# A depthwise-and-FFT block on one core: the rounding of x and layer 1's additions moved from engines into DMAs

## What is computed

```python
def layer0(x):
    xh = conv1x1(gn(x), w_in, b_in)                  # 128 -> 256 channels
    hcx = relu(mean(xh, points) @ kg_w1.T + kg_b1)   # per image
    k = (hcx @ kg_w2.T + kg_b2)                      # per image: a 3x3 kernel for each of 256 channels
    y = mish(depthwise3x3(xh, k))
    return conv1x1(y, w_out, b_out)                  # 256 -> 128
def layer1(x):                                       # fft over channels, mask, two 128x128 maps, ifft, relu
    return relu(real(ifft(complex(amp_map(fft(x) * mask), phase_map(...)))))
x = x + layer0(x)
x = x + layer1(gn(x))
```

## Time and profile before

| | |
|---|---|
| median of the runs | 3897.72 us |
| profiled execution | 3897.35 us, its span 3895.3 us |
| TensorE busy | 3759.3 us, 97% |
| VectorE busy | 3525.0 us, 90% |
| ScalarE busy | 3448.4 us, 89% |
| GpSimd busy | 2632.5 us, 68% |
| DMA engines busy | 29.5% for the one queue that SyncE issues to |

### The profile page before, as it was taken

One profiled execution on the slowest core, in us unless ns is written; L12 is line 12 of the kernel. 1 busy time (PEld: TensorE's weight loads), 2 busy tenths in 40 slices (PEclk: granted clock), 3 DMA queues, 4 the chain that ended last, 5 costly groups with the idle time before them and its releaser, 6 DMA issues.

```text
span 3895.3 us, 65845 instructions
## 1 busy us (share of the span) xinstructions
PE 3759.3 (97%) x22348; PEld 2259.9 (58%) x22348; DVE 3525.0 (90%) x4778; ACT 3448.4 (89%) x5604; POOL 2632.5 (68%) x2132
## 2 busy tenths in 40 slices
PE   4899999999999999999999999999999999999998
PEld 2555655656555555555556555565655556556554
DVE  5899989899998989989899898998989899899996
ACT  4988999898998989989899998999989999898875
POOL 3456676776767767677777767767677776777763
PEclk8999999999999999999999999999999999999999
DMA  3112333333233333333333332333333233231223
GB/s 139 64 46 85 109 108 110 103 109 114 98 114 103 109 109 105 113 104 109 103 112 111 104 110 102 112 111 103 109 104 113 105 109 111 103 113 71 74 73 124
DMA packets 111292, 401.86 MB, mean 103 GB/s; under 512 B 13232, under 2 KB 14320, under 8 KB 110704
## 3 DMA queue, kind: packets, MB, share of 16 engines
q1 hardware_dynamic: 110960, 397.66, 29.5%
HBM read 263.39 MB, written 134.22 MB: 102 GB/s over the span
## 4 chain that ended last, share of the span: by engine, by line
PE 77%; ACT 7%; POOL 4%; issue 3%; DVE 2%; ACTq 0%; POOLq 0%
PE psA L657 35%; PE psBO L703 19%; PE psL L712 9%; PE psBO L681 2%; PE psBO L683 2%; PE psBO L682 2%; ACT tprod L413 2%; POOL tsum L1110 2%; PE psBO L692 1%; ACT XS L454 1%; PE psBO L694 1%; PE psBO L693 1%; ACT xh L386 1%; PE psA L666 1%; DVE accS L924 1%
## 5 line engine op out<-in xcount | busy, mean ns | idle before, releaser
L657 PE MATMUL psA<-hi,wa 128*128 128x288 f16 (+4 forms) x9792 | 1938.6, 280 | 0.8 <-DVE wtmp L881 0.8
L912 DVE SCALAR_TENSOR_TENSOR accB<-xh,vectors,accB 128x1024 f32<-128x1024 f32 x1280 | 1640.1, 1281 | 0.0
L1110 POOL TENSOR_TENSOR tsum<-tsum,tprod 128x1024 f32<-128x1024 f32 x512 | 1210.6, 2364 | 315.9 <-ACT tprod L413 315.9
L924 DVE SCALAR_TENSOR_TENSOR accS<-side,vectors,accS 128x448 f32<-128x448 f32 x2048 | 1398.6, 683 | 24.1 <-ACT accS L422 14.9
L657 PE MATMUL psA<-lo,wa 128*128 128x288 f16 (+5 forms) x4896 | 1322.0, 280 | 0.0
L657 PEld LDWEIGHTS psA<-hi,wa 128*128 128x128 f16 x9792 | 926.8, 98 | 328.7 <-issue 63.0
L703 PE MATMUL psBO<-wm,woutt 128*128 128x512 f32 x2048 | 963.2, 593 | 3.6 <-DVE X L934 2.1
L1114 POOL TENSOR_TENSOR X<-X,zt 128x512 f32<-128x512 f32 x480 | 612.4, 1276 | 464.3 <-DVE accB L912 394.7
L1102 POOL TENSOR_TENSOR lo<-X,hi 128x1024 f16<-128x1024 f32 x256 | 547.6, 2139 | 359.2 <-ACT hi L371 356.9
L703 PEld LDWEIGHTS psBO<-wm,woutt 128*128 128x128 f32 x2048 | 386.5, 190 | 482.4 <-issue 481.0
L413 ACT ACTIVATE tprod<-xh,vectors 128x1024 f32<-128x1024 f32 x512 | 583.6, 1140 | 31.4 <-POOL tsum L1110 29.4
(11 more groups left out here) (166 smaller groups left out, 3434.6 us busy)
## 6 DMA issues: line engine op xcount, KB each, us to landing
X<-in_x_dram SPq DMA_DIRECT2D x256, 512.0 KB, 3.3
out_dram<-X SPq DMA_DIRECT2D x256, 512.0 KB, 2.6
XS<-in_x_dram SPq DMA_DIRECT2D x240, 512.0 KB, 3.3
X<-in_w_t_dram SPq DMA_DIRECT2D x2, 1152.0 KB, 17.6
w1t<-in_w_t_dram SPq DMA_DIRECT2D x1, 256.0 KB, 2.8
wint<-in_w_in_t_dram SPq DMA_DIRECT2D x1, 128.0 KB, 2.3
woutt<-in_w_out_t_dram SPq DMA_DIRECT2D x1, 128.0 KB, 2.8
wm<-in_cos_m_dram SPq DMA_DIRECT2D x1, 64.0 KB, 4.1
```

The lines of the kernel that those rows point to most:

```text
L657: last = mm(o[:, r:r + q, 0:cols], w, src[:, at:at + q, SIDE + dx - 1:SIDE + dx - 1 + cols], start=(tap == ORDER[0] and w is wh and src is ...
L912: V.scalar_tensor_tensor(out=rows_of(accB[:]), in0=xh[:, 8 * j + dy:8 * j + dy + 8, dx:dx + W], scalar=kk[i % 2][:, TAPS + k:TAPS + k + 1] ...
L924: V.scalar_tensor_tensor(out=side_out(), in0=side[:, 8 * j + dy:8 * j + dy + 8, dx:dx + SIDE], scalar=kk[i % 2][:, k:k + 1], in1=side_out( ...
L1110: P.tensor_tensor(tsum[:], tsum[:], tprod[:], ALU.add).then_inc(s_ta, 1)
```

## The change

Four things are changed.

1. `hi` is no longer made by ScalarE. GpSimd issues a DMA (`high`) that reads the strip from memory once more and rounds it to float16 on the way into `hi`. ScalarE's `cast` is gone.
2. GpSimd's `cast`, which makes `lo`, is done for strip n+3 in place of n+2, and stands behind the second `tap_add` of the slot in place of behind the first `add`. Three strips are done ahead of the loop.
3. GpSimd's `add` becomes a DMA that adds `zt` to the stored strip in memory. SyncE's `store` therefore comes three slots after the strip, as soon as the residual is done; `load_x` waits for the store and for layer 1's matmul. `relu` waits for the landing of the accumulation of the strip before.
4. The building of the next image's weights is set one strip earlier up to the kernels, and its matmuls change banks: group means at strip 9, root at 10, pooled products and hidden layer at 11, kernels at 12 (in `small_1`), bias rows at 14 (in `small_0`), one spread in each of 13, 14 and 15 (in `small_1`). `pool_bias` stands behind `tap_add` and `high`. Seven slots in place of six carry two statistics strips.

```diff
 def stat_strips(n):
-    if n < 6:
+    if n < 7:
         return (2 * n, 2 * n + 1)
-    return (n + 6,) if n + 6 < STATS else ()
+    return (n + 7,) if n + 7 < STATS else ()
...
 def load_x(n):
     ...
         eng.wait_ge(s_out[m % 4], 16 * (m // 4 + 1))
+        eng.wait_ge(s_lm, 2 * m + 2)
...
 def store(m):
-    eng.wait_ge(s_add, 2 * m + 2)
+    eng.wait_ge(s_x1, 2 * m + 2)
...
-                if n >= LAG1 + 1:
-                    store(n - LAG1 - 1)
+                if 3 <= n < N - STRIPS + 3:
+                    store(n - 3)
...
 def relu(m, t):
     ...
     if m >= 1:
-        eng.wait_ge(s_add, 2 * m + t - 1)
+        eng.wait_ge(s_acc[t], 16 * m)
...
+def high(n):
+    b, s, j = n // STRIPS, n % STRIPS, n % 4
+    if n >= 3:
+        eng.wait_ge(s_cv, 2 * (n - 3) + 1)
+    if n >= 4:
+        eng.wait_ge(s_xm, 3 * (n - 4) + 3)
+        eng.wait_ge(s_lo, n - 3)
+    eng.dma_start(hi[:, 8 * j:8 * j + 8, :].rearrange("p r c -> p (r c)"),
+                  x[b, :, s * SP:(s + 1) * SP]).then_inc(s_hi[j], 16)
...
 def add(m, t):
+    b, at = m // STRIPS, m % STRIPS * SP + t * TP
     eng.wait_ge(s_re, 2 * m + t + 1)
-    P.tensor_tensor(half(m, t), half(m, t), zt[:, t, :], ALU.add).then_inc(s_add, 1)
+    eng.wait_ge(s_out[m % 4], 16 * (m // 4 + 1))
+    eng.dma_start(out[b, :, at:at + TP], zt[:, t, :], accum_op=ALU.add).then_inc(s_acc[t], 16)
...
 # GpSimd's slot(n)
     if m >= 1:
         add(m - 1, 1)
-    if n + 2 < N:
-        cast(n + 2)
     ...
     if n + 1 < N:
         tap_add(n + 1, 1)
+    if n + 3 < N:
+        high(n + 3)
+    if s == 11 and build:
+        pool_bias(b + 1)
     if m >= 0:
         add(m, 0)
     if n + 1 < N:
         for k in range(2, EXTRA + 1):
             tap_add(n + 1, k)
+    if n + 3 < N:
+        cast(n + 3)
+    if s == 9 and build:
+        variance("x", b + 1, s_px)
     if s == 10 and build:
-        variance("x", b + 1, s_px)
-    if s == 11 and build:
         rstd("x", b + 1, s_px)
         fold(b + 1)
     ...
     if s == 2 and b >= 1:
         rstd("1", b - 1, s_p1)
         fold_1(b - 1)
```

## The result

| | before | after |
|---|---|---|
| median of the runs | 3897.97 us | 3945.65 us |
| profiled execution's span | 3895.3 us | 3945.0 us |
| VectorE, ScalarE, GpSimd busy | 90%, 89%, 68% | 93%, 82%, 67% |
| DMA engines busy, bytes moved | 0.29, 102 GB/s | 0.64, 151 GB/s |

The changed kernel is slower: the ratio is 1.0125, with an interval of 1.0107 to 1.0142. That is +48 us where +30 was forecast, and inside the range.

The account below looks back on a forecast made before the run. TensorE was taken to bound the ordinary slot at 14.15 us. Per-batch terms +28, the loop +3, additions +2 and first image −3 made +30 on 3897.35, so 3927 us; range for 8 in 10 runs 3885 to 4085.

Parts of the forecast that it names:

- What bounds the kernel: Ordinary slots: TensorE is busy for all 14.15 us, so taking work from ScalarE or GpSimd can't shorten them.
- GpSimd's order: `cast` ahead of the inverse root makes it 2.13 us later; TensorE waits: strip 3 +1.05, strip 11 +1.37.
- the wait for `pool_bias`: Before the hidden-layer matmul: `pool_bias` behind `tap_add` and a DMA issue costs +0.6 us, or nothing for d of 0.4 or less.
- The size of the waits: Strips 3, 12, 13, mostly before the side product: 4.0 us per batch, 59 us or 1.5% at most to gain.
- The small products: Moving the kernel matmuls to strip 12 saves strip 13's 1.85 us; bias rows at strip 14 add 0.7 us.
- The issue price d: GpSimd's time to issue one DMA, three per slot: taken as 1.0 us, within 0.33 to 2.13.
- the loop: From VectorE's first tap through GpSimd's sums, two issues and `cast` back: 12.17 + 2d, passing 14.15 at d = 0.99; +3 us.
- The first rival: The loop binds ordinary slots, with issue at 1.3 us or landing at 4.9: 4040 us, chance 0.27.
- The lock between VectorE and GpSimd: VectorE's first tap and GpSimd's `cast` do not run side by side: the whole 2.13 us charged, possibly only 1.4.
- Additions as DMAs: 480 GpSimd additions of 1.27 us become DMAs: DMA engines 0.64 busy, room enough; +2 us behind the loop.
- Start and first image: Startup roundings cost 0, up to +4 us; first image −3, five slots 0.94 shorter and a seventh statistics slot +1.9.
- The rival of the relief: ScalarE's relief decides if GpSimd reaches the root no later than now: waits go, −48 us, 3850 us; chance 0.10.

Follow-up runs that it names:

- e4: The kernel before with only the rounding DMA for the upper half of x in place of ScalarE's rounding; 3855.11 us, ratio 0.9885.
- the lengthened kernel: The changed kernel with five tiny GpSimd operations between the rounding and first accumulation issues in strips 4 to 8; 4025.23 us, ratio 1.0340.
- e7: e2 with five tiny GpSimd operations added between the same two issues in strips 4 to 8; 3858.62 us, ratio 0.9904.
- e2: The changed kernel with GpSimd's lower-half pass back behind the slot's first accumulation, for strip n+2; 3863.32 us, ratio 0.9907.
- e1: The changed kernel with the inverse root and fold put ahead of GpSimd's lower-half pass at strips 2 and 10; 3866.43 us, ratio 0.9915.

## Why the prediction was right, and where it was off

The forecast's way and most of its terms held; the result lies 18.7 us above it because one term was missing, and one of the agreements is luck in part.

- **What bounds the kernel**: held. Ordinary slots stayed at 14.15 us in every kernel whose loop was not lengthened, whatever ScalarE, VectorE, GpSimd and the DMA engines had to do.
- **GpSimd's order**: held. The root was forecast 2.13 us later with TensorE standing for it in both places; TensorE stood 2.08 and 2.07 us. Strip 3 was to be +1.05 and was +1.0 where the clock held. Strip 11 was to be 1.37 + 0.6 above the strip 12 of before (1.97) and was 18.03 - 16.11 = 1.92. That agreement is luck in part: the relief taken off, 0.76, was 0.46 by e4, and the wait for `pool_bias` before the hidden layer's matmul, put at 0.6, was 0.15 us of idle at most in these 14 images; the two errors nearly cancel.
- **The term that was missing** is the clock behind the stall: 19.9 us at strip 3 and 2.9 at strip 11. I priced an idle TensorE at the idle time and no more. In the trace of before no such stall stood in an ordinary image, so no row showed it. These 22.8 us are more than the whole difference between forecast and result (18.7); without them the span would have grown by 26.9, against +30. That the time still lies inside the range is owed to the range's width.
- **The size of the waits**: read from slot lengths they came to 4.0 us per batch, 59 us in all. The rounding DMA alone took away 0.95 + 0.46 + 1.48 = 2.9 us and left no idle above 0.15 us in those strips, so some 43 us was the most, and the other quarter was no wait.
- **The small products**: strip 13's wait went; by e4 it was 1.48 and not 1.85. The 0.7 us for the bias rows at strip 14 did not come: strip 14 took 15.29 with no idle listed, 0.2 less than before, with one spread less in it. The wait is there without ScalarE's relief, at 1.0 rather than the 1.6 that I had (1.08 + 0.55), and the 0.94 covers it. Strips 9 to 15 together were to be +0.8 per image and were +0.5 without the clock (9.9 - 2.9 = 7.0, over 14).
- **The issue price d**: taken as 1.0 with bounds of 0.33 and 2.13. The line views of the changed kernel, rounding and accumulation (ns min/median/max):

```profile
L1084 POOL DMA_DIRECT2D hi<-in_x_dram x256: 577/612/749, 12.3 to 3838.0; - x128
...
DMA to landing us min/median/max: 3.5/4.1/12.1
```

```profile
L1109 POOL DMA_DIRECT2D out_dram<-zt x480: 853/895/960, 362.7 to 3900.4; - x160
...
DMA to landing us min/median/max: 3.8/4.9/8.0
```

  Two issues are 1.5 us, not 2.0, so the loop is 13.7 by my terms (13.5 by the lengthened kernel) and the 3 us for it fell away. The landing of 4.1 us leaves 9.85 + 4.1 = 13.95, just inside the slot. The first rival was closer than its time suggests: 0.65 us more in the loop and it binds. The Trainium skill, "DMA: Bandwidth & Descriptors", section "Latency and other measured facts", gives about 1 us to first byte for GpSimd's path. No view here shows a first byte; for the price of an issue on the engine the measured 0.61 and 0.90 decide.
- **The lock between VectorE and GpSimd**: charged in full, and the tap does wait for nearly all of the pass (in the lengthened loop it ends 1.10 us past the pass's end, and takes 1.28 alone). The Trainium skill, "SBUF — State Buffer", section "SBUF: two separate sides", says that a VectorE operation with two SBUF inputs, such as the tap, and a GpSimd operation that reads SBUF exclude one another for the whole instruction; the trace agrees.
- **Additions as DMAs**: nothing in the loop, +2 behind it forecast; +2.8 measured with that part alone, +1.3 in the changed kernel.
- **Start and first image**: the start was taken as 0 and was +3.9. The kernels with the rounding DMA have +3.8 to +4.8, those without +0.1 to +0.9. The sixteen first strips land 13.5 us after their issue in place of 9.5, beside three more strips; TensorE's first group means wait 22.5 us for the statistics in place of 18.4. The first image was -1.9, with -3 forecast.
- **The rival of the relief** had its condition right: "if GpSimd reached the root no later than now". With the root put ahead it gave 3866, with the rounding alone 3855; the rival's time was 3850.

What stays open: why an idle time of some 2 us brings the clock down in 12 of 15 images at strip 3, in one of 14 at strip 11, and in 9 of 14 at strip 11 of the lengthened kernel. The length of the idle time alone does not separate them: at strip 3 the clock fell after 1.90 us and held after 2.17, and at strip 11 of the lengthened kernel, where it is 2.06 to 2.55, the clock fell after 2.07 and held after 2.38. That e7 is 4.7 us faster than e2 with five operations more needs no cause of its own so far: 3.7 us of it is the difference of the kernel before in the two groups, and the ratios, 0.9904 and 0.9907, do not tell the two apart.

## What to carry to other kernels

Where a step is moved on an in-order engine, find the short serial chain that stands behind its new place and who waits for its end: here 2 us ahead of fifteen tiny operations turned a gain of 1% into a loss of 1.2%. Price a stall of TensorE above its idle time, since the clock can fall behind it: here for 1.6 us more where nothing else waited, and for 0.65 and 0.97 where the slower TensorE filled a wait for ScalarE. And take a change with several parts apart by waits: one part held all of the gain, one nearly all of the loss, and the other two were worth nothing or cost a little.

## What was not expected of the hardware

- After about 2 us in which TensorE ran nothing, its granted clock fell to half for some 3.5 us, in 12 of 15 images at one place; the slot grew by 1.6 us beside the stall's own 1.0. In the two kernels in which the stall is gone and the DMAs are the same (e1, e2) no strip 3 or 11 of the last 15 and 14 images had a clock below 1.00.
- The DMA engines' busy share more than doubled (0.29 to 0.64, 102 to 151 GB/s); that lengthened landings (x strips 3.3 to 4.9 us) and no ordinary slot of the loop.
- Adding to a stored half strip by DMA, 256 KB, takes GpSimd 0.90 us of issue and lands in 4.9 us; rounding a strip on the way in takes 0.61 and 4.1 us.
